# Zero products at the start, another order of the first two batches' stages, and later maxima, in a one-core decoder layer

## What is computed

```python
x = x + attention(layernorm(x))         # 32 heads of 64, 8 key/value heads, rotary, causal softmax, wo
x = x + q8(layernorm(x)) @ q8(ctx)      # both sides rounded to fp8 steps, scaled by maxima of 128-blocks
x = x + moe(layernorm(x))               # 8 experts, capacity 256, hidden 704, plus a shared expert
```

## Time and profile before

| | us |
|---|---|
| median of 3 runs (lowest, highest) | 1531.96 (1529.91, 1532.4) |
| the profiled execution, its own time | 1527.53 |
| its span | 1525.4 |
| PE busy (share of the span) | 1435.0 (94%) |
| DVE busy | 1164.8 (76%) |
| ACT busy | 973.8 (64%) |
| POOL busy | 1030.9 (68%) |

### The profile page before, as it was taken

How to read it: one execution, slowest core, us unless ns; L and a number is a source line. 1 busy time by engine, 2 the same in 40 slices (tenths; PEclk the granted TensorE clock), 3 DMA queues, 4 the chain that set the end, 5 groups by cost and what they waited for, 6 DMA issues and landing times.

```text
span 1525.4 us, 26946 instructions
## 1 busy us (share of the span) xinstructions
PE 1435.0 (94%) x8617; PEld 1264.6 (83%) x8617; DVE 1164.8 (76%) x2810; ACT 973.8 (64%) x2510; POOL 1030.9 (68%) x1057
## 2 busy tenths in 40 slices
PE   5999999999999999799999999888899899999997
PEld 3788888888878888688878878777788888999996
DVE  7688888887888887888888888888576753677773
ACT  4687777777677788578877777765142412555562
POOL 3787898887877889689889978754313131366663
PEclk9999999999999999999999999999999999999999
DMA  6445544334322433324334342603111011587772
GB/s 211 136 111 173 158 111 136 113 86 121 88 84 57 124 101 91 86 78 128 85 94 130 81 123 63 181 10 124 57 41 44 21 43 40 174 264 237 252 245 82
DMA packets 108620, 174.74 MB, mean 115 GB/s; under 512 B 20936, under 2 KB 42696, under 8 KB 108480
## 3 DMA queue, kind: packets, MB, share of 16 engines
q1 hardware_dynamic: 104448, 160.51, 36.3%
q0 software_dynamic: 3840, 12.25, 2.1%
q10 hardware_dynamic: 192, 0.26, 0.1%
HBM read 94.05 MB, written 33.18 MB: 83 GB/s over the span
## 4 chain that ended last, share of the span: by engine, by line
PE 73%; DVE 10%; ACT 9%; issue 4%; DMA 2%; POOL 1%; SPq 1%; DVEq 0%; POOLq 0%; ACTq 0%
PE bank L514 16%; PE bank L516 16%; PE bank L515 16%; PE bank L566 7%; PE bank L532 4%; PE bank L581 4%; PE bank L582 4%; PE bank L533 4%; ACT P L912 3%; DVE PTl L1297 2%; PE bank L506 2%; DVE Zb L1358 1%; ACT Otmp L918 1%; ACT PTh L924 1%; DVE P L1256 1%
## 5 line engine op out<-in xcount | busy, mean ns | idle before, releaser
L912 ACT ACTIVATE P<-P,mn 128x512 f32<-128x512 f32 (+3 forms) x512 | 284.1, 561 | 173.8 <-DVE mn L1256 173.4
L1695 POOL TENSOR_TENSOR P<-P,ri 128x128 f32<-128x128 f32 (+3 forms) x512 | 358.0, 730 | 35.0 <-DVE ri L1245 34.9
L1256 DVE CUSTOM_DVE_ANT_0 P<-bank,mask 128x512 f32<-128x512 f32 (+3 forms) x512 | 228.3, 482 | 84.2 <-PE bank L533 83.2
L1297 DVE TENSOR_TENSOR PTl<-bank,PTh 128x512 fp32r<-128x512 f32 (+1 forms) x384 | 210.0, 595 | 5.2 <-ACT PTh L924 1.3
L924 ACT ACTIVATE PTh<-bank 128x512 fp32r<-128x512 f32 (+1 forms) x384 | 176.1, 528 | 21.7 <-PE bank L566 18.4
L532 PE MATMUL bank<-KT,QT 128*128 128x256 f32 (+2 forms) x512 | 166.1, 334 | 19.9 <-DVE mn L1256 19.9
L514 PE MATMUL bank<-XT,Wh 128*128 128x512 f32 x384 | 163.4, 426 | 8.3 <-DVE XT L1227 3.5
L566 PE MATMUL bank<-ident,P 128*128 128x128 f32 x1280 | 169.3, 276 | 0.2 <-POOL P L1695 0.2
L581 PE MATMUL bank<-PTh,VS 128*128 128x256 f32 (+2 forms) x512 | 161.4, 326 | 8.1 <-issue 3.1
L533 PE MATMUL bank<-KT,QT 128*128 128x256 f32 (+2 forms) x512 | 161.6, 324 | 0.0
L582 PE MATMUL bank<-PTl,VS 128*128 128x256 f32 (+2 forms) x512 | 155.4, 325 | 0.0
(11 more groups left out here) (229 smaller groups left out, 4131.4 us busy)
## 6 DMA issues: line engine op xcount, KB each, us to landing
RW<-in_wf SPq DMA_DIRECT2D x153, 256.0 KB, 3.6
QT<-qh SPq DMA_DIRECT2D x256, 64.0 KB, 2.0
QT<-ql SPq DMA_DIRECT2D x252, 64.0 KB, 2.0
Oraw<-in_wo SPq DMA_DIRECT2D x16, 512.0 KB, 4.7
KT<-KT SPq DMA_DIRECT2D x32, 256.0 KB, 3.1
Wraw<-in_wqkv SPq DMA_DIRECT2D x9, 768.0 KB, 5.1
xnx<-in_ctx SPq DMA_DIRECT2D x24, 256.0 KB, 3.7
saved<-Wh SPq DMA_DIRECT2D x7, 768.0 KB, 3.5
```

The costliest lines, as they stand in the source:

```text
L912: e.activation(pq, pq, ACT.Exp, bias=mn[:, z, qb:qb + 1], scale=-1.0, accum_out=rs[:, z, qb:qb + 1]).then_inc(a_exp, 1)
L1256: e.tensor_tensor_reduce(P[:, z, off[qb]:off[qb] + k], bank[n % 2][:, 0:k], mask[:, 512 - k:512], -0.125, BIG, ALU.add, ALU.min, mn[:, z, ...
L1297: e.tensor_tensor(pt_part(PTl, part), bank[2 + part][:, 0:128 * n].rearrange("p (m n) -> p m n", n=128), pt_part(PTh, part).bitcast(F32), ...
L1695: e.tensor_tensor(pq, pq, ri[:, z, qb:qb + 1].to_broadcast([128, n]), ALU.mult).then_inc(g_norm, 1)
```

## The change

Seven edits. (1) PE runs eight products of a zeroed tile with itself (128x512, plain fp32) into bank 7 before anything else. (2) POOL waits for the four normed tiles before its first split of weights. (3) The split of the first output weights (`split_wo(0)`, ACT, DVE, POOL) goes from the start to step 2. (4) ACT's statistics of batch 2 go from the start to steps 0 to 8, those of batch 3 from steps 0 to 8 to steps 9 to 17; the inverse roots that follow move by two steps. (5) ACT takes the high parts of tiles 4 to 7 ahead of `query_hi(0)`, and issues its four query transfers after `key_hi(0)` and `split_wq(1, 0)`. (6) POOL does `rotate_key(0)` ahead of `query_lo(0)`. (7) `look` moves on by one step on both engines, on DVE also from the head of the step to after `split_wo_lo`, ahead of the mask of query block 1 (the third of the step); `first_scales` moves by one step.

```diff
 # PE
+            def idle_products(n):
+                need.wait_ge(g_zero, 1)
+                for _ in range(n):
+                    e.matmul(bank[7][:, :], Zb[:, 0, 0:128], Zb[:, 0, :], start=True, stop=True)
...
+            idle_products(8)
             for t in range(TB):
                 first_turn(t, t)
 # ACT
             for t in range(TB):
                 first_turn(t, t)
-            split_wo(0, 0)
-            split_wo(0, 1)
-            for t in range(2 * TB, 3 * TB):
-                tile_sum(t)
-            tile_means(2)
-            for t in range(2 * TB, 3 * TB):
-                tile_squares(t)
             values_keys(0)
-            query_hi(0)
             for t in range(TB, 2 * TB):
                 first_turn(t, t - TB)
+            query_hi(0)
             value_hi(0)
-            place_queries(e, need, 0, 1, (0, 1))
             key_hi(0)
             split_wq(1, 0)
+            place_queries(e, need, 0, 1, (0, 1))
             split_wq(1, 1)
...
+                if h == 2:
+                    split_wo(0, 0)
+                    split_wo(0, 1)
...
-                for b, at in ((3, 0), (0, 64)):
+                for b, at in ((2, 0), (3, 9), (0, 64)):
...
-                if 77 <= h < 81:
-                    look(h - 77)
+                if 78 <= h < 82:
+                    look(h - 78)
 # DVE
             for t in range(TB, 2 * TB):
                 first_stats(t)
-            split_wo_lo(0)
             for fn in range(2):
                 rotate(0, 0, fn)
...
-                if 78 <= h < 82:
-                    look(h - 78)
-                if h == 83:
+                if h == 84:
                     first_scales()
...
+                if h == 2:
+                    split_wo_lo(0)
                 if h >= 15 and h % 8 == 7 and h // 8 < NEP:
                     split_wo_lo(h // 8)
+                if 79 <= h < 83:
+                    look(h - 79)
                 if 0 <= h < NH:
                     masked(h, 1)
                     masked(h, 0)
...
-                if h == 17:
+                if h == 19:
                     need.wait_ge(a_sq, 2 * TB)
 # POOL
+            need.wait_ge(v_xn, TB)
             split_wq_lo(0, 0)
             split_wq_lo(0, 2)
-            split_wo_lo(0)
             rotate(0)
+            rotate_key(0)
             query_lo(0)
-            rotate_key(0)
             key_lo(0)
...
+                if h == 2:
+                    split_wo_lo(0)
...
-                for n, at in enumerate((18, 22, 26, 73, 74, 75)):
+                for n, at in enumerate((20, 24, 28, 73, 74, 75)):
```

## The result

| | us |
|---|---|
| forecast | 1526.3 (1514 to 1531) |
| the changed kernel, median of 20 runs (lowest, highest) | 1538.54 (1529.2, 1546.06) |
| the kernel before, 20 runs beside it | 1534.93 (1525.72, 1540.22) |
| ratio, 95% interval | 1.0032 [1.0017, 1.0047] |
| the profiled execution after, its own time, its span | 1534.95, 1532.7 |

The change makes the kernel some 3.6 us slower; the forecast was 5.7 us faster. The 12 us between forecast and result have two parts. 3.0 us are the base: 1531.96 was the median of three runs, 1534.93 is that of twenty. The other 9.3 us are the error that the rest of the document is about.

What follows compares the result with a forecast made beforehand. PE bounds the kernel (busy 319.9 of 320 us from 95 to 415), so gains ahead of it are kept. Start 5.4, less 0.3 in steps 0 to 17, plus 0.6 maxima: 5.7 off 1532.0 gives 1526.3 us, range 1514 to 1531.

Steps and rivals of the forecast that it cites:

- The failed step: Behind the maxima: steps taken as unchanged; forecast wrong if steps 77 to 127 differ by more than 3 us.
- Rival B: Steps 78 to 84 or later pass pairs: a new DVE stall against POOL, up to 11.2 us, 1537.5; chance 0.09.
- the stall of step 77: DVE's tensor-scalar pass of 9.89 us at 610.57, with PE standing 7.8 us; expected again, near 9.9 us.
- S: Start of `project(0)` on PE: from 16.8 to 14.4 us, gain 2.4, between 14.0 and 15.2.
- The products: PE's start: eight zero products, at most 0.94 us each, hidden by 8.8; raise the clock, little on the path.
- S to head 0: From the start of `project(0)` to head 0: 25.9 us instead of 28.9, the keys' landing deciding; head 0 at 40.3.
- `split_wo` in step 2: Steps 0 to 17: the moved output-weight split delays POOL's keys; cost 0 to 2.7 us, taken as 0.3.
- The maxima: Steps 78 to 85: later `look` hides DVE's 3.6 us wait for ACT; net gain 0.6, bounds -1.5 and +2.5.
- A: Step 77: its long DVE pass goes or comes by chance; if it goes, 1515.1 us; chance 0.14.
- C: Start: products hold the transposes or the clock falls again; head 0 at 45.7 at worst, 1531.7 us; chance 0.15.

Runs made afterwards that it cites:

- e1: The changed kernel with `look` and `first_scales` back at their old steps, all other edits kept: 1535.51 us, ratio 1.0001.
- e10: The kernel before with one empty wait added on POOL ahead of its first weight split: 1541.11 us, ratio 1.0037.
- e13: The kernel before with POOL's third memset split in two halves, one instruction more and no more work: 1542.55 us, ratio 1.0055.
- e6: The kernel before, unedited, traced a third time: single run 1534.73 us.
- experiment 5: POOL waits before `pair` in fourth steps until DVE's next-step `steps_of` or `large_steps_of` is done: 1513.7 us on the kernel before, 1506.77 on the changed one.
- e9: The changed kernel without POOL's wait for the four normed tiles: 1534.59 us, ratio 1.0.
- e12: e4 without the eight zero products on PE: 1508.79 us, ratio 0.9841.
- e4: The changed kernel with POOL waiting before `pair` in fourth steps until DVE's next-step `steps_of` or `large_steps_of` is done: 1506.77 us, ratio 0.9815.
- e3: The kernel before with POOL waiting before `pair` in fourth steps until DVE's next-step `steps_of` or `large_steps_of` is done: 1513.7 us, ratio 0.985.
- e14: The changed kernel with POOL's third memset split in two halves: 1529.66 us, ratio 0.9973.

## Why the prediction was wrong

**The failed step** is the one that said nothing changes behind step 84: "the shift constant to step 77" was right, but the forecast also took steps 85 to 127 as unchanged, and named as its own refutation a difference of over 3 us there. It was 7.8 us in step 117. Rival B had this kind of stall, with a chance of 0.09 and a price of up to 11.2 us ("or any of the 12 pairs of passes behind"); its price here was 7.8. But I tied it to edit 7 and its new timing, and the runs show that edit 7 has no part in it (e1, e10, e13): it is the one instruction that edit 2 adds to POOL. Nor is B's condition, POOL without a gap for over 8.8 us, what decides: in e6 POOL has no gap of more than 0.2 us from 930.04 to 951.12, and DVE's pass gets in at 938.97 all the same.

**What misled me.** Of the stall of step 77 I wrote that the code up to it is unchanged, that PE paces all engines, and so that it stays. It did, to 0.02 us. I carried the same argument over to all later steps: same code, same pace, same stalls. But their timing has a part that the code of the step doesn't hold, the number of instructions ahead of it on POOL. With gaps of 0.3 us deciding between 0.74 and 6.86 us, taking these steps as unchanged would have needed the same count.

**The base.** The profile had no long pass at step 89, which all twelve other profiles without the waits of experiment 5 have. Its 1527.53 us, 4.4 below the median of three runs and 7.4 below that of twenty, was the sign, and I only subtracted it away.

**The terms of the sum:**

- *S*: forecast 14.4, measured 15.01, inside 14.0 to 15.2. The norms took 1.92 us (forecast 1.9); the products, ending at 11.28 instead of 8.8, cost the 0.6 (in e1, where they end at 10.06, S is 14.45). My upper bound for a product, 0.94 us, holds only for the last of them (0.86); the first cost 1.7.
- *Edit 2* was put at 1.9 us (norms ending at 11.5 instead of 13.4), and is worth 1.8 to 2.1 at the norms, also where POOL's splits hold two of the small passes instead, which I had not seen. The 3.3 us at head 0 of e9 contain a late input too.
- *The products* were put at little on the path; at head 0 no gain of theirs can be told (e12).
- *S to head 0*: 25.6 against 25.9, with the keys' landing last, as forecast. That head 0 comes within 0.3 us of the forecast is in part luck, since S is 0.6 late and the way from it 0.3 short. Gain at head 0 5.1 us in the first profile and 5.3 over three; forecast 5.4.
- *`split_wo` in step 2*: the shift falls to 3.7 us at step 4, and is 6.2 at step 8 of the first profile: it is made good where step 5 stands for `xnx<-in_ctx` (5.51 us in the chain). Forecast 0.3 in all.
- *The maxima*: DVE's wait for ACT went from 3.6 to 0.6 us, as forecast, and no time came of it: steps 78 to 85, which the prediction named, took 64.9 us in all three profiles of before and 65.8, 66.3 and 65.8 after. Expected -0.6, measured +1.0, inside the bounds but with the wrong sign. The first profiles' steps 78 to 82 took 39.9 and 40.8. Where no stall of step 77 stands ahead, these steps are 39.2 us (e4) against 41.7 (e3); which edit does that is not told apart.
- *Rivals A and C* did not come: the pass of step 77 stayed, and the start did what it says.

**What stays open.** What POOL does at each 128th instruction was not shown. The page lists a queue for instructions:

```profile
q14 instruction: 70, 0.57, 0.1%
```

0.57 MB in 70 transfers is 8.1 KB each, 64 bytes for each of 128 instructions; and a transfer of this queue follows each of five pauses (one in e14, two in after, two in e10) by 0.6 to 0.9 us. That POOL goes over to the next block of its program there is my inference; 70 blocks are far more than POOL's 1348 records fill, so the queue can't be POOL's alone, and record 315 speaks against a pause at each block. Open too is how a shift of 0.3 us becomes a stall: the pauses at 827 and 955 and the long pass of step 117 come together in seven traces and are missing together in nine, but the way from one to the other was not followed. Open too is why a pass is passed over for several instructions. In steps 77, 81, 89, 113 and 117 each long pass began within 0.03 us of a wait record of POOL's, and the free ones of step 117 some 0.35 us ahead of one; but the pass of step 98 doesn't fit that, and moving that wait alone was not tried.

## What to carry to other kernels

A kernel of engines in tight lockstep can have steps in which 0.3 us decide over 7: before such a kernel is tuned at one end, list its longest single instructions against their usual time, and take those stalls away first (here 21 us for a wait of POOL's, and the tuned start then shows its worth). Count an added instruction, even an empty wait, as a shift of everything behind it on that engine; when a change is right at its place and wrong in the total, look for the first later step whose length differs, and try the change with one empty instruction more. And profile the base more than once: here the profile that lay well below the median lacked a stall that the other executions have.

## What the runs showed of the hardware

- A DVE pass of 0.4 us can take 3.5 to 9.9 us beside POOL; the one of 6.86 us was passed over for five POOL instructions. Passes on four columns (0.16 us) are held too, each for one POOL instruction (1.17 to 1.20 us).
- POOL pauses some 0.3 us at three places 128 records apart in its program (699, 827, 955), seen where it has just been waiting; at record 315, also behind a wait, it does not.
- A true fp32 product of 128x512 took 1.7 us and, later in the same row, 0.86; an fp32r one takes 0.43 and 0.23 at the two levels of the clock.
- In two kernels one instruction longer on POOL, with no work added, the whole kernel is 6.2 and 8.5 us slower.
